# Two norms from one variance in a two-layer decoder: both roots in one power, both normalised rows from x

## What is computed

```python
def _layernorm(x, axis=-1, eps=1e-05):
    ...
    return (x - m) / jnp.sqrt(v + eps)
# first layer, its argument is _layernorm(x): EPS = 1e-05
h = _ln(x, ln1_g, ln1_b)          # (x - m) * rsqrt(var + EPS) * g + b
x = x + ob @ w_out + b_out
# third layer, its argument is _layernorm(x): EPS = 1e-06
h = rmsnorm(X, norm1_w)           # x * rsqrt(mean(x * x) + EPS) * w
X = X + ctx @ wo
```

## Time and profile before

| | us |
|---|---|
| median of 3 runs | 1434.56 (1434.55 to 1436.48) |
| profiled execution | 1429.93 |
| its span | 1428.1 |
| PE busy | 1273.5 (89%) |
| DVE busy | 853.7 (60%) |
| POOL busy | 638.7 (45%) |
| ACT busy | 570.3 (40%) |

### The profile page before, as it was taken

The page is one execution under the profiler, slowest core; times in us unless marked ns, Lnnn a source line. Parts: engine busy times, 40 slices in busy tenths (PEclk is TensorE's granted clock), DMA queues, the critical chain, the costliest instruction groups (busy, mean ns, idle before and its releaser), DMA issues.

```text
span 1428.1 us, 35852 instructions
## 1 busy us (share of the span) xinstructions
PE 1273.5 (89%) x13189; PEld 1066.0 (75%) x13189; DVE 853.7 (60%) x2071; ACT 570.3 (40%) x1272; POOL 638.7 (45%) x885
## 2 busy tenths in 40 slices
PE   5999879989999999989999999689989999549895
PEld 4777658977777788768989999667767887448674
DVE  4888833348888788757311121379866788744335
ACT  2555545424444555633222222135444555314220
POOL 4455531036664455620233333268764444355253
PEclk9999989989999999999999999899999999869997
DMA  6000000020000000001699999510000000069933
GB/s 258 3 2 0 2 31 1 1 93 17 16 12 2 9 17 11 20 9 45 228 327 317 344 333 325 186 54 27 8 13 20 24 30 17 18 199 356 278 101 111
DMA packets 47376, 137.88 MB, mean 97 GB/s; under 512 B 6925, under 2 KB 29646, under 8 KB 41104
## 3 DMA queue, kind: packets, MB, share of 16 engines
q1 hardware_dynamic: 32944, 110.37, 22.0%
q0 software_dynamic: 7536, 19.67, 4.4%
q10 hardware_dynamic: 6768, 6.16, 1.3%
HBM read 119.54 MB, written 17.56 MB: 96 GB/s over the span
## 4 chain that ended last, share of the span: by engine, by line
PE 55%; DVE 22%; issue 9%; POOL 5%; DMA 5%; ACT 2%; DVEq 0%; SPq 0%; POOLq 0%; ACTq 0%
PE ps L1118 10%; PE ps L1352 10%; PE ps L1036 7%; DVE negmax L1794 6%; PE ps L1364 5%; PE ps L1080 4%; PE ps L1060 3%; PE ps L981 3%; DMA row_in<-rows_of,from_u 3%; PE ps L984 2%; PE ps L922 2%; PE ps L1087 2%; DVE u L1760 2%; PE ps L969 1%; POOL gn L887 1%
## 5 line engine op out<-in xcount | busy, mean ns | idle before, releaser
L1418 ACT ACTIVATE probsT_all<-ps 128x1024 f32<-128x1024 f32 x128 | 131.1, 1024 | 165.1 <-PE ps L984 165.1
L1794 DVE TENSOR_REDUCE negmax<-ps 128x8 f32<-128x1024 f32 x128 | 156.0, 1218 | 45.7 <-PE ps L981 45.3
L1352 PE MATMUL ps<-hT,w_tile 128*128 128x128 f32 x1304 | 164.6, 281 | 10.7 <-issue 5.3
L1352 PEld LDWEIGHTS ps<-hT,w_tile 128*128 128x128 f32 x1304 | 156.6, 197 | 14.0 <-issue 13.2
L984 PE MATMUL ps<-qe,kf 32*128 32x256 f32 x1280 | 151.4, 384 | 0.0
L981 PE MATMUL ps<-kf,qe 32*128 32x128 f32 x2048 | 146.8, 282 | 0.0
L981 PEld LDWEIGHTS ps<-kf,qe 32*128 32x128 f32 x2048 | 128.2, 188 | 1.6 <-issue 0.8
L758 POOL TENSOR_SCALAR eps_sum<-mv 128x1 f32<-128x1 f32 x112 | 25.4, 227 | 220.5 <-DVE mv L1731 131.0
L984 PEld LDWEIGHTS ps<-qe,kf 32*128 32x128 f32 x1280 | 109.5, 187 | 3.9 <-issue 2.7
L2356 DVE TENSOR_TENSOR h_in<-ps,act_sb 128x512 f32<-128x512 f32 x39 | 27.0, 692 | 140.0 <-PE ps L1352 126.5
L1411 ACT ACTIVATE hT<-ps,vecs 128x128 f32<-128x128 f32 x142 | 47.1, 385 | 143.7 <-PE ps L1337 118.6
(11 more groups left out here) (287 smaller groups left out, 3232.0 us busy)
## 6 DMA issues: line engine op xcount, KB each, us to landing
w_tile<-in_w_f SPq DMA_DIRECT2D x29, 1536.0 KB
w_tile<-in_w_f SPq DMA_DIRECT2D x47, 385.0 KB
y_back<-in_w_f SPq DMA_DIRECT2D x10, 1536.0 KB
back_of<-w_odd ACTq DMA_DIRECT2D x47, 128.0 KB
ctxT<-in_ctxT SPq DMA_DIRECT2D x32, 128.0 KB, 2.0
rows_of<-nv SPq DMA_DIRECT2D x32, 128.0 KB, 1.7
w_even<-in_w_att SPq DMA_DIRECT2D x3, 1024.0 KB, 7.0
y_back<-back_of SPq DMA_DIRECT2D x6, 512.0 KB, 5.4
```

The source lines that it names most:

```text
L1352: last = mm(ps[:, 2 * which + at.two, fc * P:(fc + 1) * P], w[:, col:col + P], rowT[:, at.two, c, :], start=c == 0, stop=c == KC - 1)
L1418: nc.scalar.activation(half_of(probsT_all, half), ps[:, 2:4].rearrange("p b n -> p (b n)"), ACT.Exp, scale=HD ** -0.5).then_inc(S["probs"], 1)
L1794: nc.vector.tensor_reduce(m, ps[:, 0:2].rearrange("p b (h k) -> p (b h) k", h=HB), AX.X, ALU.max, negate=True).then_inc(S["s_max"], 1)
```

## The change

ATT0 and ATT1 no longer measure a second variance. POOL makes two sums from the one variance, a second tensor_scalar giving var·(1+e2)+1e-5·e2, and one power over the two columns gives both factors. DVE writes u and v one behind the other, both from x, with the same mean. The semaphores var2 and rstd2 go. `norm_root` and the three single calls of `inverse_root` for XATT0 and RET are changed only in how they name the buffer and in their arguments.

```diff
-SOME = {"var2": TWO_NORMS, "rstd2": TWO_NORMS, "v_norm": TWO_NORMS, "base_sb": SOFTMAX, ...
+SOME = {"v_norm": TWO_NORMS, "base_sb": SOFTMAX, ...
...
-            "dve_ln": (2, 1, 1, 1, 1), "dve_nm": (4, 1, 1, 0, 1),
+            "dve_ln": (1, 1, 1, 1, 1), "dve_nm": (4, 1, 1, 0, 1),
...
-        eps_sum = sb("eps_sum", [P, 2, 1])
+        eps_sum = sb("eps_sum", [P, 2, 2])
...
-            def inverse_root(tile, which, p):
-
-                var_, eps = ("var1", 1e-5) if which == 0 else ("var2", 1e-6 if tile.l == ATT1 else 1e-5)
-                wait_apart(pool, (var_, reached(var_, tile)))
-                nc.gpsimd.tensor_scalar(eps_sum[:, p], mv[:, p, 1:2], eps, None, ALU.add).then_inc(S["pool_r"], 1)
-                wait(pool, "pool_r", tile, which + 1)
-                nc.gpsimd.tensor_tensor(rstd[:, p, which:which + 1], eps_sum[:, p], half_neg[:, 0:1],
-                                        ALU.pow).then_inc(S["rstd1" if which == 0 else "rstd2"], 1)
+            def inverse_root(tile, p):
+
+                first, second = 1e-5, 1e-6 if tile.l == ATT1 else 1e-5
+                n = increments("pool_r", tile.l)
+                wait_apart(pool, ("var1", reached("var1", tile)))
+                nc.gpsimd.tensor_scalar(eps_sum[:, p, 0:1], mv[:, p, 1:2], first, None, ALU.add).then_inc(S["pool_r"], 1)
+                if n == 2:
+                    nc.gpsimd.tensor_scalar(eps_sum[:, p, 1:2], mv[:, p, 1:2], 1.0 + second, first * second, ALU.mult,
+                                            ALU.add).then_inc(S["pool_r"], 1)
+                wait(pool, "pool_r", tile)
+                nc.gpsimd.tensor_tensor(rstd[:, p, 0:n], eps_sum[:, p, 0:n], half_neg[:, 0:n], ALU.pow).then_inc(S["rstd1"], 1)
...
             def step(at):
...
-                    inverse_root(at[3], 0, at[3].p)
+                    inverse_root(at[3], at[3].p)
...
                 norm_root(normed(at))
-                if 3 in at:
-                    if at[3].l in TWO_NORMS:
-                        inverse_root(at[3], 1, at[3].p)
                 if 2 in at:
...
-            def second_variance(tile):
-                p = tile.p
-                wait(dve, "u_norm", tile)
-                if tile.l == ATT0:
-                    moments(u[:, p], p, "var2", "dve_ln", reached("dve_ln", tile, 2))
-                elif tile.l == ATT1:
-                    nc.vector.tensor_tensor_reduce(v[:, p], u[:, p], u[:, p], 1.0 / D, 0.0, ALU.mult, ALU.add,
-                                                   mv[:, p, 1:2]).then_inc(S["var2"], 1)
-
             def second_norm(tile):
                 p = tile.p
                 if tile.l in TWO_NORMS:
-                    wait(dve, "rstd2", tile)
-                    if tile.l == ATT0:
-                        ts(v[:, p], u[:, p], mv[:, p, 0:1], rstd[:, p, 1:2], ALU.subtract, ALU.mult).then_inc(S["v_norm"], 1)
-                    else:
-                        ts(v[:, p], u[:, p], rstd[:, p, 1:2], None, ALU.mult).then_inc(S["v_norm"], 1)
+                    ts(v[:, p], x_tile(tile.t), mv[:, p, 0:1], rstd[:, p, 1:2], ALU.subtract, ALU.mult).then_inc(S["v_norm"], 1)
...
                     normalise(first[0])
-                    if first[0].l in TWO_NORMS:
-                        second_variance(first[0])
+                    second_norm(first[0])
...
                 if to_max:
                     maxima(to_max, 0)
-                if 3 in at:
-                    second_norm(at[3])
                 if 1 in at:
                     values(at[1])
```

More of the change, by code:

```diff
@@ L158 @@
 SOFTMAX = (ATT0, XATT0, ATT1, XATT1)
-SOME = {"var2": TWO_NORMS, "rstd2": TWO_NORMS, "v_norm": TWO_NORMS, "base_sb": SOFTMAX, "swapped": ROTARY,
+SOME = {"v_norm": TWO_NORMS, "base_sb": SOFTMAX, "swapped": ROTARY,
         "zmax_sb": (ATT0,), "zero_exp": (ATT0,), "pad_mask": (XATT0,), "pad_in": (XATT0,), "gn_var": (RET,),
@@ L367, in sem @@
             return S[name]
-        for name in ("var1 rstd1 u_norm var2 rstd2 v_norm base_sb uT_out hT_sb qk_out v_out qk_sb swapped rotated o_sb centred qe_sb va_sb "
+        for name in ("var1 rstd1 u_norm v_norm base_sb uT_out hT_sb qk_out v_out qk_sb swapped rotated o_sb centred qe_sb va_sb "
                      "s_out s_max st_out probs pv_out nm_sb m_out inj_sb zero_exp o_norm oT_out oT_sb y_out x_done "
@@ L820, in norm_root @@
                 per, eps = (1.0 / D, 1e-6) if f == MOE0 else (1.0, 1e-5)
-                nc.gpsimd.tensor_scalar(eps_sum[:, p], mv[:, p, 1:2], per, eps, ALU.mult, ALU.add).then_inc(S["pool_n"], 1)
+                nc.gpsimd.tensor_scalar(eps_sum[:, p, 0:1], mv[:, p, 1:2], per, eps, ALU.mult, ALU.add).then_inc(S["pool_n"], 1)
                 pool.wait_ge(S["pool_n"], n_reached("pool_n", f, tile.t))
-                nc.gpsimd.tensor_tensor(rstd[:, p, 0:1], eps_sum[:, p], half_neg[:, 0:1], ALU.pow).then_inc(S["n_rstd"], 1)
+                nc.gpsimd.tensor_tensor(rstd[:, p, 0:1], eps_sum[:, p, 0:1], half_neg[:, 0:1], ALU.pow).then_inc(S["n_rstd"], 1)
             def norm_base(tile):
@@ L864, in step @@
                 if 3 in at and not first_crossed(at[3]) and not (at[3].l == RET and isinstance(at[3].t, int) and at[3].t == 2):
-                    inverse_root(at[3], 0, at[3].p)
+                    inverse_root(at[3], at[3].p)
                     if at[3].l == RET and isinstance(at[3].t, int) and at[3].t == 1:
-                        inverse_root(tiles_of(RET, 2), 0, 0)
+                        inverse_root(tiles_of(RET, 2), 0)
                 norm_root(normed(at))
-                if 3 in at:
-                    if at[3].l in TWO_NORMS:
-                        inverse_root(at[3], 1, at[3].p)
                 if 2 in at:
@@ L898, in _ @@
             pool.wait_ge(S["late_in"], 80)
-            inverse_root(tiles_of(XATT0, 0), 0, 0)
+            inverse_root(tiles_of(XATT0, 0), 0)
             pool.wait_ge(S["acc_done"], units("acc_done", MLP, F_EXPERTS[MLP] - 1, GROUPS - 1, GT))
```

## The result

The changed kernel takes 1445.61 us (median of 5 runs, 1441.66 to 1447.79) against 1434.55 us before (5 runs). The ratio is 1.0089, with an interval of 1.0064 to 1.0113: slower by 9 to 16 us. A second set of runs of the same kernel gave 1.0077 (1.0050 to 1.0103). The forecast was slower, 1448.3 us, in a range of 1440 to 1452.

What follows compares the result with a forecast made beforehand. The prediction took DVE's stretch from u to the first maximum to bound ATT0 and ATT1. ATT0 7.0+0.3−1.8=+5.5 and ATT1 +8.2 gave +13.7 us, 1448.3 us against the median 1434.56, range 1440 to 1452.

Steps and rivals of the forecast that it cites:

- What bounds ATT0 and ATT1: In both layers DVE's stretch from u to the first maximum is on the path: 1.46 us in ATT0, 1.06 in ATT1.
- v on the path: ATT0: v, free between the maxima, moves straight behind u at 0.33 us; the gap it leaves buys nothing.
- The added POOL operation: POOL's roots: 0.22 us for the added tensor_scalar, two-column power taken as 0.57; both roots hidden from DVE.
- 0.15 was named as a sign: ATT0: a sign of the forecast would be POOL's queries starting within 0.15 us of u.
- The two holds in ATT0: Steps with u, v and nv: queries hold v, base holds nv; +0.64 us a step, 11 steps, +7.0 us.
- The other steps of ATT0: Five steps without nv: first four wait for PE or POOL at the maximum; the last is held once, about +0.3 us.
- The holds in ATT1: Queries hold u, base copy holds nv: +0.61 us, 11 times, +6.7; four steps without nv +0.4 each, +1.6.
- the rival of one hold: ATT0 and ATT1: nv slips in before the base, or queries hold only nv; +7.1 us, 1441.7 us; chance 0.18.
- The opening: Tile 0: v at 9.78 instead of 11.54, −1.76 us, taken whole though late weights could leave between 0 and 1.76.
- The sum: ATT0 with the opening +5.5 us and ATT1 +8.2 us make +13.7 us, 1448.3 us against the median.
- Dearer holds: Rival on every hold: its tail is a whole tensor_scalar, 0.26 us dearer on 49 holds; +26 us, 1460; chance 0.05.

Runs made afterwards that it cites:

- e7: The changed kernel once more, unaltered, for a second profile; 1445.87 us, ratio 1.0077.
- e2: The changed kernel, but in ATT0 and ATT1 POOL waits with the base (ATT1: its copy) until nv is written, queries still early; 1437.11 us, ratio 1.0008.
- e1: The changed kernel, but in ATT0 and ATT1 POOL waits with the queries until DVE has written v and any nv; 1420.12 us, ratio 0.9898.
- e3: The changed kernel, but v is written behind the first maximum again, queries still early; 1427.80 us, ratio 0.9959.
- e4: The changed kernel with v behind the first maximum and POOL's queries only after u and nv; 1417.38 us, ratio 0.9878.
- e5: The kernel of e4, with POOL's queries waiting for nv in XATT1 too; 1412.30 us, ratio 0.9836.
- e6: The kernel before, with only one wait added: in XATT1 POOL's queries wait for nv; 1431.32 us, ratio 0.9979.
- e8: The kernel before once more, unaltered, for a second profile; 1437.0 us, one run.

## Why the prediction was right, step by step

**What bounds ATT0 and ATT1.** Right. All that lay between u and the first maximum appeared in the step: 0.65 more there, 0.63 more in the step (11.35 for 10.72).

**v on the path.** Right: it follows u at 0.33 us, and the gap it left only made DVE's wait for PE longer, 1.63 for 0.88 us.

**The added POOL operation.** Hidden, but mis-sized: the power over two columns took 0.72 us, not 0.57. With the second sum (0.27 from start to start) the root for nv ended at 130.58, 0.26 us after the start of u. That moved the queries to 0.23 us behind u where 0.05 was forecast, and 0.15 was named as a sign. It changed nothing, since they still came before v.

**The two holds in ATT0.** Right, and to 0.01 us: 2.10 was forecast, 2.11 is the rule, with two steps of 2.2, in which the queries came 0.04 and 0.06 us before u and held u instead of v. Forecast 11×0.64=7.0; the 11 distances add up to 7.4 us.

**The other steps of ATT0.** Here a reading was wrong. The prediction has the first four steps without nv wait for PE or POOL at the maximum, and gives them no cost. In tile 3's step the kernel before does not wait there (1.31 us from u to the maximum, no idle time). In e7 the queries hold v in that step:

```profile
29.27 1.13 DVE L1765 TENSOR_SCALAR v<-x_all,mv,rstd 128x256 f32<-128x256 f32 x1
```

The step takes 8.91 us there for 8.42 before, and 8.91 in e2 as well, while it is 8.42 to 8.43 in e1, e3 and e4, where v is not held. That is +0.5. Tile 4 has +0.2, where 0.3 was forecast. Against them stands a gain that the prediction does not have: the step behind the last u takes 9.77 us for 10.41, because a small operation behind the second maximum is short now, before and in the changed kernel:

```profile
163.74 0.97 DVE L1815 TENSOR_SCALAR negmax<-negmax,const 128x16 f32<-128x16 f32 x1
```

```profile
170.88 0.23 DVE L1802 TENSOR_SCALAR negmax<-negmax,const 128x16 f32<-128x16 f32 x1
```

It stood beside a POOL operation of 1.28 us (L859, from 163.39), which in the changed kernel is over by then; whether it was held by it was not tried. So 7.4+0.5+0.2−0.6 make the 7.4 us that ATT0 grows without the clock spell told under the opening; 7.3 was forecast. That this agrees so well is luck of two omitted terms that cancel.

**The holds in ATT1.** The first is right (u 0.95 us, forecast 0.96). The second was forecast to hit 11 times out of 11, with a lead of 0.07 us for the copy. It hit 9 times (nv 0.48 to 0.56 us) and missed twice, where nv was ahead of the copy (0.34 us), in e7 in the same two steps; there the maximum comes 1.46 us after u instead of 1.66 to 1.74. Three more steps, with 1.50 to 1.55, had the second hold but a shorter first one. So the rival of one hold came true in 2 of 11 steps. The 11 distances add up to 17.6 us for 11.6 before, +6.0 where 6.7 was forecast; the four steps without nv took 1.10 instead of the 1.21 forecast, +1.1. The sum, 7.1 us, is nearly the whole growth of XATT0+ATT1 (7.2); 8.2 was forecast, and this is the term that was mis-sized.

**The opening.** v of tile 0 comes 1.52 us earlier, where 1.76 was forecast: u itself came 0.46 us late instead of 0.22, by the second sum (0.27) and the longer power (0.73 for 0.57). With the earlier trace rows before them:

```profile
9.69 0.41 DVE L1760 TENSOR_SCALAR u<-x_all,mv,rstd 128x256 f32<-128x256 f32 x1 [3.58 <-POOL rstd L764]
10.02 0.41 DVE L1765 TENSOR_SCALAR v<-x_all,mv,rstd 128x256 f32<-128x256 f32 x1
```

The weights, which the prediction could not place, were not in the way: PE's first matmuls with them (L1036) begin at 12.29 us for 13.82. The first maximum came 1.64 us earlier. Yet one step later only 0.4 us of that was left in this profile. The stretch of 4 us in which PE projects tile 2, in the changed kernel and then in the kernel before (busy us of PE, PEld, DVE, ACT, POOL, then granted clock, DMA share, GB/s):

```profile
25.00:29.00 4.00, 3.59 (x19) 3.37 (x21) 2.72 (x11) 0.57 (x4) 1.14 (x3) 0.61 0.65 273
```

```profile
27.00:31.00 4.00, 3.94 (x51) 3.18 (x51) 3.08 (x12) 1.35 (x5) 0.78 (x2) 1.00 0.05 18
```

In the changed kernel a part of it ran at the lower clock level of 1.2 GHz (mean 0.61), at 1.00 before. Its 16 matmuls of L1036 took 3.5 us instead of 2.2. ATT0's second step took 9.62 us, against 8.91 in e7, the same kernel, where the clock stood at 1.00 in these 4 us. So 0.7 us of the step are the clock's, which comes and goes with the execution; the other 0.5 us over the 8.42 of before are the hold of v told above, and belong to the change.

**The sum.** +13.7 us forecast, +13.7 in the layers (−1.6+8.1+7.2), +11.1 between the medians, +9 to +16 by the interval. The agreement in the layers is better than its terms: ATT0 and the opening came out 1.0 us dearer than forecast together, ATT1 1.0 cheaper, and 0.7 of ATT0 is the clock spell, without which the layers give +13.0. The mechanism was right; that the sum met 13.7 to the tenth is luck.

**Dearer holds.** Excluded: the tail behind a POOL operation is 0.14 to 0.15 us in every held u, v and nv above. The cost of a hold is what is left of the other's duration and 0.15 us, not that and a whole 0.41. The Trainium skill, SBUF — State Buffer, section Who interferes with whom, has the one block the other fully; for who waits for whom the rows agree with it (v 1.12 us beside the queries), and it gives no price for the end of the wait.

**What the layers do not show.** In e1 to e5 the totals gain 4 to 10 us more than the layers (6, 5.5, 4, 5 and 10), and the rest is 801 to 803 us for 803 to 807 in the profiles before and after. The traces show a part of it. The 8 us from 12 to 20 us after the last maximum of ATT1, where the same work begins, in the kernel before and then in e2:

```profile
611.80:619.80 8.00, 7.78 (x23) 6.21 (x24) 1.83 (x5) 1.50 (x5) 2.91 (x5) 0.57 0.10 34
```

```profile
618.75:626.75 8.00, 7.07 (x36) 5.59 (x37) 2.42 (x7) 2.98 (x10) 3.65 (x6) 1.00 0.10 34
```

Before, most of it ran at the lower level, and so it did in e6, e7, e8 and the changed kernel (0.57 in all five); in e1 to e5 it stood at 1.00. In the 8 us ahead PE was equally busy in both kernels, 3.47 and 2.48 us of each 4. The first `red` of MOE0 on DVE (L2061 before) begins 22.2 to 22.3 us after the last maximum of ATT1 with the spell and 19.1 without, 3.1 us. In e1 and e3 the stretch from ATT0's last first maximum to that of XATT0 is also 129.4 us at a mean clock of 0.96, for 132.1 to 133.2 at 0.93 to 0.94 in all others. Why the clock differs there is open: each of e1 to e5 has one profile only, and the rest of one kernel varies by 4.5 us between two profiles (before and e8). The comparison of before and after is free of these two, as both kernels have both spells.

## What to carry to other kernels

A wait that looks like waste on an idle engine can be what keeps it out of another engine's way: before removing it, look where that engine's queue will land, and look for the same meeting in a layer that never had the wait. Where two engines hold one another, put the work that can wait explicitly behind the instructions on the path; here one wait was worth more (1.06 us in a step of ATT0) than all the work removed. Work that fills a gap behind another engine's wait is free; moved onto the path it costs what it lengthens the path by. v cost 0.28 us in a step of ATT1 (9.22 in e1, 8.94 in e4) and nothing in ATT0, where PE is last in both.

## What was not expected of the hardware

A POOL power over 128x2 took 0.72 us and over 128x1 0.55 to 0.57 us, so a second column costs 0.15 us: a good quarter of a second instruction, but not nothing. And who gets in first is settled by hundredths of a microsecond: with the copy at the same recorded start as nv (524.48) nv was held, with the copy 0.10 us behind it (574.49, nv at 574.39) it was not.
